# Second cross attention with whole-array work between the transposes of a burst, and an expert stage in stretches of four blocks

## What is computed

```python
# C: 16 heads of 64, keys and values from the context of the same length
xn = _layernorm(x, ln_gamma, ln_beta)
q = (xn @ w_q).reshape(B, SQ, NUM_HEADS, DIM_HEAD)
k, v = jnp.split(context @ w_kv, 2, axis=-1)
scores = jnp.einsum('bqhd,bkhd->bhqk', q * SCALE, k)
attn = jax.nn.softmax(scores, axis=-1)
out = jnp.einsum('bhqk,bkhd->bqhd', attn, v).reshape(B, SQ, INNER)
out = out @ w_out + b_out
...
# D: 8 heads, 64 keys a half, the best 8 of each half, the best 8 of their 64 sums, out of 4096 experts
sim1 = jnp.einsum('bthd,hkd->bthk', q[..., 0, :], keys[:, :, 0, :])
sim2 = jnp.einsum('bthd,hkd->bthk', q[..., 1, :], keys[:, :, 1, :])
s1, i1 = jax.lax.top_k(sim1, K)
s2, i2 = jax.lax.top_k(sim2, K)
fs, pk = jax.lax.top_k(all_sc, K)
wd, wu = expert_down[fi], expert_up[fi]
hidden = jax.nn.gelu(jnp.einsum('btd,bthkd->bthk', xn, wd), approximate=False)
hidden = hidden * jax.nn.relu(fs)
return jnp.einsum('bthk,bthkd->btd', hidden, wu)
```

## Time and profile before

| | us |
|---|---|
| median of 3 runs (2198.76 to 2201.66) | 2201.64 |
| the profiled execution | 2201.63 |
| its span | 2199.8 |

### The profile page before, as it was taken

One profiled execution on the slowest core, in us unless ns is written; L12 is line 12 of the kernel. 1 busy time (PEld: TensorE's weight loads), 2 busy tenths in 40 slices (PEclk: granted clock), 3 DMA queues, 4 the chain that ended last, 5 costly groups with the idle time before them and its releaser, 6 DMA issues. The chain is left out here.

```text
span 2199.8 us, 44678 instructions
## 1 busy us (share of the span) xinstructions
PE 2140.0 (97%) x17740; PEld 1443.5 (66%) x17740; DVE 1671.2 (76%) x4463; ACT 791.6 (36%) x1687; POOL 270.2 (12%) x515
## 2 busy tenths in 40 slices
PE   7999989999999999999999999999999999999998
PEld 3555544446746746775556555556689989898997
DVE  6888886776576576536887787877788988889896
ACT  4877772312302302303554554555422111211210
POOL 4866643000000000000000001000000000000000
PEclk9999999999999999999999999999999999999999
DMA  5112104000000003001000000001200000000000
GB/s 181 33 46 52 34 22 158 1 1 1 1 0 1 1 1 115 1 1 51 1 1 1 1 1 1 1 1 51 94 12 2 2 11 2 1 11 1 2 11 10
DMA packets 26207, 50.66 MB, mean 23 GB/s; under 512 B 6032, under 2 KB 14480, under 8 KB 24976
## 3 DMA queue, kind: packets, MB, share of 16 engines
q1 hardware_dynamic: 26000, 47.81, 6.6%
HBM read 37.57 MB, written 2.10 MB: 18 GB/s over the span
## 5 line engine op out<-in xcount | busy, mean ns | idle before, releaser
L2423 PE MATMUL banks<-work,big 128*128 128x128 f32 x2016 | 247.5, 276 | 0.9 <-DMA big<-in_D_up 0.9
L626 ACT ACTIVATE work<-banks,work 128x512 f32<-128x512 f32 x256 | 174.8, 687 | 202.2 <-DVE work L746 202.2
L2423 PEld LDWEIGHTS banks<-work,big 128*128 128x128 f32 x2016 | 241.3, 192 | 5.9 <-DMA big<-in_D_up 1.1
L1121 PE MATMUL banks<-big,work 128*128 128x256 f32 x1024 | 241.2, 379 | 0.0
L1045 PE MATMUL banks<-big,work 128*128 128x512 f32 x512 | 226.6, 596 | 0.0
L2520 ACT ACTIVATE work<-banks 128x512 f32<-128x512 f32 x126 | 75.3, 597 | 398.5 <-PE banks L2423 398.5
L1121 PEld LDWEIGHTS banks<-big,work 128*128 128x128 f32 x1024 | 195.0, 190 | 33.9 <-issue 1.9
L1045 PEld LDWEIGHTS banks<-big,work 128*128 128x128 f32 x512 | 95.5, 190 | 113.8 <-issue 112.8
L1963 ACT ACTIVATE work<-work 128x512 f32<-128x512 f32 x256 | 164.3, 711 | 0.1
L746 DVE TENSOR_REDUCE work<-banks 128x2 f32<-128x1024 f32 x128 | 150.5, 1217 | 7.7 <-PE banks L478 7.7
L1343 DVE CUSTOM_DVE_ANT_0 work<-banks,work 128x512 f32<-128x512 f32 (+3 forms) x128 | 57.6, 488 | 121.5 <-PE banks L1061 109.4
(11 more groups left out here) (256 smaller groups left out, 3782.1 us busy)
## 6 DMA issues: line engine op xcount, KB each, us to landing
work<-work SPq DMA_DIRECT2D x168, 32.0 KB, 2.0
big<-in_bias SPq DMA_DIRECT2D x16, 256.0 KB, 3.6
big<-in_B_val SPq DMA_DIRECT2D x8, 512.0 KB, 5.4
big<-in_B_out SPq DMA_DIRECT2D x1, 4096.0 KB, 16.7
big<-in_D_downT SPq DMA_DIRECT2D x4, 1024.0 KB, 5.6
big<-in_D_up SPq DMA_DIRECT2D x1, 4096.0 KB, 15.6
wc<-in_ctxT SPq DMA_DIRECT2D x1, 2048.0 KB, 8.0
wab<-in_L_ffn_w_q SPq DMA_DIRECT2D x1, 2048.0 KB, 9.5
```

The lines of the kernel that those rows point to most:

```text
L626: eng.activation(prob[:, n % NS * PAIR + j, :], SB[n % 2][:, j, :], ACT.Exp, bias=low[:, n % NS, j:j + 1], accum_out=rowsum[:, n % NS, j:j ...
L1121: last = eng.matmul(XO[qt // 2][:, qt % 2 * D:(qt % 2 + 1) * D], spread[:, c % NG, qt * P:(qt + 1) * P], w_out[:, c, :], start=False, stop ...
L2423: last = eng.matmul(HP[n % 2][:, q * P:(q + 1) * P], down[:, (n * NJ + q) * KC + kc, :], xnT[par][:, kc, :], start=(kc == 0), stop=(kc == ...
```

## The change

In C a burst's two `scores` now come ahead of the first `turn_probs`, and all work that uses the whole array stands between the two transpositions: keys and queries together in u = 0 bursts; values, project, folded keys, transposed x and weigh together in u = 1 bursts. In the bursts of t = 5, 6, 7 and 0, `weigh` comes first and `values` after it, in bank `FB[1]` instead of `FB[0]`. ScalarE's and VectorE's lists follow: the layer norm parts of VectorE move from the head of the burst's list to just before its last copy, and both reads of keys and queries stand before the second `normalise`. In D, TensorE's turn is two halves, each with four `hidden`, two `weights`, four `spend` (and in between x and compare, or the picks), and two `weights`; VectorE's list is written out in that order.

```diff
@@ -544,10 +546,10 @@
                         values(0, 0, 1, FB[0])
                         eng.wait_ge(q_ready.sem, q_ready.at(0, 2))
                         values(0, 0, 2, FB[1])
+                    for i in range(2):
+                        scores(b, t, u, n, i)
                     if n >= 2:
                         turn_probs(n - 2)
-                    for i in range(2):
-                        scores(b, t, u, n, i)
                     if n == 0:
                         values(0, 0, 0, FB[1])
                     if n == 2:
@@ -556,51 +558,42 @@
                     after = (b, t + 1) if t < T - 1 else (b + 1, 0)
                     if u == 0 and after[0] < B:
                         keys(*after)
+                        queries(*after)
                     elif u == 0:
                         eng.wait_ge(on_ready.sem, on_ready.at(b, T - 2))
                         compare(0, FB[0])
-                    if u == 1 and b == B - 1 and t in (5, 6):
-                        eng.wait_ge(s["dq_loaded"], 32)
+                        compare(1, FB[1])
+                    elif after[0] < B:
                         eng.wait_ge(k_ready.sem, k_ready.at(*after) + 1)
-                        fold_keys(eng, m, t - 5, FB[0])
                         eng.wait_ge(q_ready.sem, q_ready.at(*after) + 1)
-                        fold_keys(eng, m, t - 3, FB[1])
-                    if u == 1:
-                        if after[0] < B:
-                            eng.wait_ge(k_ready.sem, k_ready.at(*after) + 1)
-                        if 1 <= t <= 4 and b == 0:
-                            eng.wait_ge(q_ready.sem, q_ready.at(b, t + 2))
-                            values(b, 1, t - 1, FB[1])
-                        elif 1 <= t <= 4:
-                            values(b, 1, t - 1, FB[0])
-                        elif t >= 5 and b < B - 1:
-                            values(b + 1, 0, t - 5, FB[0])
-                        elif t == 0 and b > 0:
-                            values(b, 0, QT - 1, FB[0])
-                        if b > 0 and 1 <= t <= 4:
-                            eng.wait_ge(q_ready.sem, q_ready.at(b, t + 2))
+                    if u == 1 and 1 <= t <= 4:
+                        values(b, 1, t - 1, FB[0 if b else 1])
+                        if b:
                             project(b - 1, t - 1, FB[1])
-                        if b < B - 1 and t in (5, 6):
+                            eng.wait_ge(v_ready.sem, v_ready.at(b, t + QT))
+                    if u == 1 and t in (5, 6):
+                        if b < B - 1:
                             turn_x(b + 1, t - 5)
+                        else:
+                            eng.wait_ge(s["dq_loaded"], 32)
+                            fold_keys(eng, m, t - 5, FB[0])
+                            fold_keys(eng, m, t - 3, FB[1])
+                            eng.wait_ge(e.fold_ready, 2 * (t - 5) + 1)
+                    if u == 1 and t == T - 1 and b == B - 1:
+                        eng.wait_ge(e.sim_ready.sem, e.sim_ready.at(0, 1))
+                        eng.wait_ge(on_ready.sem, on_ready.at(b, T - 2))
+                    if u == 1 and t:
+                        weigh(b, t - 1)
+                    elif u == 1 and b:
+                        weigh(b - 1, T - 1)
+                    if u == 1 and t >= 5 and b < B - 1:
+                        if t < T - 1:
+                            eng.wait_ge(xt_ready.sem, xt_ready.at(b + 1, t - 4))
+                        values(b + 1, 0, t - 5, FB[1])
+                    if u == 1 and t == 0 and b:
+                        values(b, 0, QT - 1, FB[1])
                     if n >= 2:
                         turn_probs(n - 1)
-                    if u == 0 and after[0] < B:
-                        queries(*after)
-                    elif u == 0:
-                        compare(1, FB[1])
-                    if u == 1 and (b or t):
-                        if b == B - 1 and t in (5, 6):
-                            eng.wait_ge(e.fold_ready, 2 * (t - 5) + 1)
-                        if b == B - 1 and t == T - 1:
-                            eng.wait_ge(e.sim_ready.sem, e.sim_ready.at(0, 1))
-                        if (b < B - 1 or t <= 4) and not (b == 0 and 1 <= t <= 4):
-                            eng.wait_ge(v_ready.sem, v_ready.at(b, t + QT))
-                        elif t == T - 1:
-                            eng.wait_ge(on_ready.sem, on_ready.at(b, T - 2))
-                        if t:
-                            weigh(b, t - 1)
-                        else:
-                            weigh(b - 1, T - 1)
 
                 for n in (B * STEPS - 2, B * STEPS - 1):
                     turn_probs(n)
@@ -677,36 +670,35 @@
                     if n == 2:
                         take_values(0, 0, 1, FB[0])
                         take_values(0, 0, 2, FB[1])
+                    spread_probs(n, 0)
+                    spread_probs(n, 1)
                     if n >= 2:
                         take_probs(n - 2)
-                    spread_probs(n, 0)
-                    spread_probs(n, 1)
                     if n == 0:
                         take_values(0, 0, 0, FB[1])
                     if n == 2:
                         take_values(0, 0, 3, FB[0])
-                    if u == 1:
-                        if 1 <= t <= 4:
-                            take_values(b, 1, t - 1, FB[0 if b else 1])
-                        elif t >= 5 and b < B - 1:
-                            take_values(b + 1, 0, t - 5, FB[0])
-                        elif t == 0 and b > 0:
-                            take_values(b, 0, QT - 1, FB[0])
+                    spread_probs(n + 1, 0)
+                    if b == B - 1 and (t, u) == (T - 1, 0):
+                        take_sims(0, FB[0])
                     if u == 1 and b == B - 1 and t in (5, 6):
                         take_fold(t - 5, FB[0])
                         take_fold(t - 3, FB[1])
-                    if b == B - 1 and (t, u) == (T - 1, 0):
-                        take_sims(0, FB[0])
-                    spread_probs(n + 1, 0)
-                    if n >= 2:
-                        take_probs(n - 1)
                     spread_probs(n + 1, 1)
                     if b == B - 1 and (t, u) == (T - 1, 0):
                         take_sims(1, FB[1])
+                    if u == 1 and 1 <= t <= 4:
+                        take_values(b, 1, t - 1, FB[0 if b else 1])
                     if u == 1 and t:
                         take_out(b, t - 1)
                     elif u == 1 and b:
                         take_out(b - 1, T - 1)
+                    if u == 1 and t >= 5 and b < B - 1:
+                        take_values(b + 1, 0, t - 5, FB[1])
+                    if u == 1 and t == 0 and b:
+                        take_values(b, 0, QT - 1, FB[1])
+                    if n >= 2:
+                        take_probs(n - 1)
@@ -794,6 +786,20 @@
                 eng.wait_ge(bo_loaded, 16)
 
                 for b, t, u, n in bursts():
+                    after = (b, t + 1) if t < T - 1 else (b + 1, 0)
+                    lowest(n)
+                    lowest(n + 1)
+                    if n >= 2:
+                        take_probs(n - 2)
+                    normalise(n)
+                    if u == 0 and after[0] < B:
+                        take_keys(*after)
+                        take_queries(*after)
+                    if u == 1 and b < B - 1 and t in (5, 6):
+                        take_x(b + 1, t - 5)
+                    normalise(n + 1)
+                    if u == 1 and b > 0 and 1 <= t <= 4:
+                        update(b - 1, t - 1, FB[1])
                     if b < B - 1 and (t, u) in NORM:
                         if b == B - 2 and (t, u) == NORM[0]:
                             eng.wait_ge(late_added, QT)
@@ -807,23 +813,8 @@
                             eng.wait_ge(turn_done.sem, turn_done.at(2, QT))
                         for part in SECOND.get((t, u), ()):
                             e.norm.on_vector(eng, 2, part)
-                    after = (b, t + 1) if t < T - 1 else (b + 1, 0)
-                    if n >= 2:
-                        take_probs(n - 2)
-                    lowest(n)
-                    lowest(n + 1)
-                    if u == 0 and after[0] < B:
-                        take_keys(*after)
-                    normalise(n)
-                    if u == 1 and b > 0 and 1 <= t <= 4:
-                        update(b - 1, t - 1, FB[1])
-                    if u == 1 and b < B - 1 and t in (5, 6):
-                        take_x(b + 1, t - 5)
                     if n >= 2:
                         take_probs(n - 1)
-                    if u == 0 and after[0] < B:
-                        take_queries(*after)
-                    normalise(n + 1)
                 take_probs(B * STEPS - 2)
                 largest(eng, m, 0)
                 take_probs(B * STEPS - 1)
@@ -2463,25 +2454,23 @@
```

(93 more changed lines are left out.)

## The result

The changed kernel takes 2214.07 us (median of 3 runs, 2211.49 to 2214.24) against 2201.64 before: ratio 1.0058, 95% interval 1.0044 to 1.0072. It is slower, and above the range of the prediction. Its profiled execution took 2211.49, around a span of 2209.7, 9.9 more than the span before.

What follows compares the result with a forecast made beforehand. The prediction took TensorE's queue as the bound from the attention to the last store. From 2201.6 us, attention -5.8 (-10.7 - 12.9 - 1.7 + 6.6 + 12.0 + 0.9) and experts +3.6 (-4.1 + 4.7 + 2.95) gave 2199.4, range 2187 to 2211.

Steps and rivals of the forecast that it cites:

- no clock term enters: TensorE's clock is granted in full in the kernel before, so the forecast charged nothing for a lower clock.
- with the same prices: Attention, u = 1 bursts: each half/whole/half array trip saved is worth 0.20, as in u = 0 bursts; 12.9 us gained together.
- The u = 0 bursts: Attention: burst falls from 6.89 to 6.56 with keys and queries together, gain 0.34; 31 bursts give 10.7 us.
- End of the attention: Last bursts, with three transpositions in a row and a late last weigh: 0.9 us lost.
- Steady turns: Experts: seven places where the next block is 0.08 longer become four, 0.25 to 0.3 a turn; fourteen turns gain 4.1 us.
- the start: First attention bursts (n = 0 to 4), where TensorE waits 1 to 2 us at a time for evictions: 1.7 us gained.
- the waits for the late copy: Attention: TensorE's transposition in u = 1 bursts waits for VectorE's last copy; 18.6 us lost, 6.6 chain and 12.0 norm parts.
- both end turns of D: Experts' first and last turns, where nothing covers the moved work: turn 0 loses 4.7 us, turn 15 loses 2.95.
- the norm parts: Attention, u = 0 bursts: VectorE's layer norm parts, now before the last copy, add in full to TensorE's wait; 12.0 us.
- the second (the copy isn't felt): Rival in the attention: VectorE's late copy starts early enough that 18.6 us of waiting go, giving 2180.8 us; chance 0.25.
- The third: Rival: nothing is won at a switch between half and whole array; 2207 to 2217 us, middle 2212; chance 0.1.
- The fourth: Rival: VectorE's list is longer than walked, each u = 0 burst waits 0.5 instead of 0.22; 2207.8 us; chance 0.15.

Runs made afterwards that it cites:

- old end turns: The changed kernel with turns 0 and 15 of the experts in the old order on TensorE and VectorE; 2199.84 us, ratio 1.0001 against the kernel before.
- copy first: The changed kernel with VectorE's copy of the second transposition, in u = 0 bursts, ahead of the second normalise and layer norm parts; 2195.69 us, ratio 0.9975 against the kernel before.

## Why the prediction was wrong, step by step

The waits were those of the prediction; two steps of it failed, and two terms were mis-sized, all to the same side. By the profiles the change is 9.9, the sum had -2.2; the 12.1 between them are (the two large ones first):

**The clock, 5.1 us, priced at nothing.** The prediction said that the clock is granted in full and that no clock term enters. That was read from the kernel before, where TensorE hardly stands still, and then kept for a kernel into which the sum itself had put two idle stretches of 5 to 6 us. Behind them the rows show 0.84 + 2.47 for picks and weights instead of 0.50 + 1.41 (1.4) and 2.55 + 8.24 instead of 1.41 + 7.0 (2.4), and at the end of C 1.05 + 3.02 instead of 0.64 + 2.11 (1.3). The first two are shown by filling the idle time. The third rests on the comparison of profiles: of the six profiles with the new order at the end of C five have the long hidden block (all but that of the old end turns), and of the three with the old order none.

**Leaving the whole array, u = 1 bursts, 5.2 us.** The step that failed is "with the same prices". I had charged every saved trip with 0.20. The u = 0 bursts bore that out: S 0.10, K 0.10 (1296.31 less 1294.48 is 1.83 instead of 1.92), Q 0.10 (1.81 instead of 1.91) and T 0.05 make 0.35. In the u = 1 bursts the block that loses its T is V or P and its new successor is W. V lasted 1.92 before T and lasts 1.92 before W; P lasted 3.55 before T and lasts 3.55 before W:

```profile
1053.52 1.98 PE L465 MATMUL banks<-big,wc 128*128 128x512 f32 x4
1055.43 3.65 PE L509 MATMUL banks<-big,wc 128*64 128x512 f32 x16
```

So only S (0.10) and T (0.59 instead of 0.64) give anything, 0.15 to 0.16 a burst instead of 0.3 with V or P, 0.13 instead of 0.4 with X, 0.71 instead of 0.85 at t = 7 and 0. The folded keys last 3.72 before T and 3.72 before W, so those two bursts give 0.15 and 0.06 instead of 0.3 (the second has two transpositions of D's x behind its T, which then takes 0.64). Without the waits the 30 bursts give 7.7, not 12.9. The lengths without waits are those of the run "copy first": 8.42 with V, 11.87 with V and P, 9.00 with X. The rows held the price for a 128x512 block before its like, never for one before W, whose tile is 128x64; that unseen pair needed a bound from nothing to 0.1, which the sum didn't have. Nor is it the successor alone. At the start of C keys and queries stand between blocks of their own kind (K, Q and V in the changed kernel), and there they take 1.72:

```profile
1014.64 1.88 PE L436 MATMUL banks<-wc,big 128*128 128x512 f32 x4
1016.36 1.88 PE L458 MATMUL banks<-work,big 128*128 128x512 f32 x4
1018.08 3.60 PE L465 MATMUL banks<-big,wc 128*128 128x512 f32 x8
```

So such a block pays 0.10 on each side where its neighbour is of another kind: 1.82 as the first behind T and 1.81 as the last before T, 1.92 with T on both sides. W counts as another kind on either side of V (T V W 1.92, W V T 1.91), P behind V does not (T V P 1.82). Why W does and why P pays before neither T nor W, no run here tells.

**End of the attention, 0.7 beside its clock.** From the last burst's W over the hidden block to the next weigh it takes 10.97 (1553.72 to 1564.69), against 8.12 before (1554.78 to 1562.90): 2.9 more. With the clock's 1.3 taken out, 1.6 is left where the walk had 0.9. The two waits for copies are those of the walk (T to T 1.73 and 1.59, taken as 1.62); which of its smaller steps was short I haven't separated.

**Steady turns, 0.8.** A turn takes 38.25 (1651.46 to 1689.71) instead of 38.48, and the experiment with the old end turns gives 3.3 for fourteen, instead of 4.1. The rest is small: 0.45 in the u = 0 bursts, 0.1 at the start, and 0.1 the other way in the waits.

What was right: the u = 0 bursts, 10.25 of gain for 30 (10.7 for 31); the start, 1.57 (1.7); the waits for the late copy, 18.5 by the lengths of the bursts (18.6), with 0.20 in a plain burst (0.22) and 0.93 more behind a stats part (0.95); V's wait for the values' x, none; W's for ScalarE, gone; the lag of turn 0 absorbed by turn 1; and both end turns of D. That each wait came out near its forecast is the walk through VectorE's list at the lengths of the earlier trace rows; that their sum is right to 0.1 us is in part luck. A T that has waited takes 0.64 and not 0.59, so a plain burst loses 0.25 (7.5 in all, where the sum had 6.6), and the norm parts cost 11.0 (12.0). The same walk named the mend: it ends in a copy that stood behind a normalise with which it had nothing to do.

Of the rivals, the second (the copy isn't felt) was wrong for this kernel, and where the copy is indeed not felt ("copy first") the time is 2195.7 and not its 2180.8, for much the same missed terms: the clock, the blocks before W, and the folds. The third gave 2212, which is near the measured time, for a reason that didn't happen: K to Q takes 1.83 where it needed 1.9 (the 1.72 that the prediction set against it was too low by its own sum, 3.64 for K and Q, which is what they take), two whole-array blocks together do gain, and by the rule of the Trainium skill that it went by (the same page, Part 3) the u = 0 bursts would have gained nothing in place of 10.25. The fourth needed 0.45 per burst and found 0.20. A time that fits a rival's number is no evidence for it; the rows that it names are.

The range was too narrow for a plain reason: its upper end was made of rivals of the attention, and the experts' two stalls had no bound of their own. The three falls of the clock alone move the forecast to 2204.5 and the upper end to 2216, and the measured time inside.

One thing stays open: the medians differ by 12.4 and the profiled executions by 9.9. The profiled execution of the changed kernel is the fastest of its three. A fold burst at the lower clock, seen in other profiles of this C and worth 3.3, would be enough for the gap, but no 2214 us execution was profiled.

## What to carry to other kernels

When a sum puts an idle stretch into TensorE's queue, price the blocks behind it at the lower clock too, even if the kernel before ran these stages at the full clock (1.00 over 1000 to 2199 here). Before reordering the bottleneck's blocks, walk the eviction engine's list and give every copy that frees a bank its place ahead of work that nobody waits for: here that one line was worth 13.5 us of the profiled attention and 0.0083 of the time. An order made for the middle of a pipeline should leave its first and last turns alone, where nothing covers what it moves.

## What the hardware showed beyond expectation

- A block's length depends on both neighbours, and not only by how much of the array each uses: 4 records of 128x512 (two float32 matmuls) take 1.72 between two blocks of their kind, 1.81 to 1.83 with a transposition of 64 rows on one side and their kind or P on the other, and 1.91 to 1.92 between two blocks of the other kind, a transposition or W; 16 records of 128x256 take 3.55 before a transposition and before W.
- Filling idle time with useless matmuls made the experts 3.8 us faster (605.4 instead of 609.2).
- Behind two waits of 1.0 and 0.9, with one transposition between them, the granted clock fell (0.66 over 1560 to 1565), though not in every execution: behind waits of 1.02 and 0.88 it stayed at 1.00 in the run with the old end turns.
- `fold_keys` and the weigh behind it ran at the lower level in some executions and not in others of the same code (3.72 + 3.6 or 5.40 + 5.17). The wait ahead was 0.96 in both. What decides it is open.
